# The second expert layer's routing for seven of eight chunks of tokens, made inside the last pass of a recurrence

## The reference: what is computed

```python
x = x + _L0_attn_a_ref(_layernorm(x), ...)       # retention
x = x + _L0_ffn_ref(_layernorm(x), Wg, bg, w1, w2)   # experts, first time
x = x + _L0_attn_b_ref(_layernorm(x), ...)       # recurrence
x = x + _L0_ffn_ref(_layernorm(x), Wg, bg, w1, w2)   # experts, second time
```

```python
logits = t @ Wg.T + bg
topw, topi = jax.lax.top_k(jax.nn.softmax(logits), 2)
```

## Time and profile before

| what | value |
|---|---|
| time, median of 3 runs | 1299.88 us (1298.88 to 1305.9) |
| the profiled execution's own time | 1299.14 us |
| its span (first to last instruction) | 1297.3 us |
| mean granted PE clock | 0.942 of full |
| busy: PE, DVE, ACT, POOL | 1118.2, 853.3, 616.5, 599.1 us |
| the last full pass of the recurrence (n = 7), from its first masked scores | about 976 to 1005 us |
| ffn2: start, first gather, first expert matmul | 1021.6, 1063.8, 1068.6 us |

### The profile page before, as it was taken

One profiled execution on the slowest core, in us unless ns is written; L12 is line 12 of the kernel. 1 busy time (PEld: TensorE's weight loads), 2 busy tenths in 40 slices (PEclk: granted clock), 3 DMA queues, 4 the chain that ended last, 5 costly groups with the idle time before them and its releaser, 6 DMA issues. The chain is left out here.

```text
span 1297.3 us, 35874 instructions
## 1 busy us (share of the span) xinstructions
PE 1118.2 (86%) x14378; PEld 828.5 (64%) x14378; DVE 853.3 (66%) x1705; ACT 616.5 (48%) x1165; POOL 599.1 (46%) x604
## 2 busy tenths in 40 slices
PE   6999999874999997879898999999886748999960
PEld 4778787653788887545555555555555537888860
DVE  4667776677555555576978888697763584555547
ACT  4666666352333332254665747366552523333324
POOL 4556565222577774506244151524411215777750
PEclk9999999996999998999999999899997969999985
DMA  8342320059533333000010101010000484333338
GB/s 304 125 156 75 123 84 34 2 196 328 178 103 103 105 101 97 33 34 4 34 35 3 34 4 34 3 35 3 3 2 3 164 322 134 103 106 103 102 119 343
DMA packets 50687, 125.54 MB, mean 97 GB/s; under 512 B 7648, under 2 KB 26848, under 8 KB 47712
## 3 DMA queue, kind: packets, MB, share of 16 engines
q1 hardware_dynamic: 36896, 86.00, 18.4%
q0 software_dynamic: 13632, 37.24, 8.8%
HBM read 79.44 MB, written 43.78 MB: 95 GB/s over the span
## 5 line engine op out<-in xcount | busy, mean ns | idle before, releaser
L1154 POOL DMA_INDIRECT ffn_xs<-xn_rows,ffn_from_row x142 | 138.4, 975 | 109.9 <-DVE ffn_second_y_at L1558 67.2
L1162 POOL DMA_INDIRECT y_rows<-ffn_ys,ffn_to_row x142 | 140.2, 987 | 68.3 <-DVE ffn_ys L1599 36.0
L1328 PE MATMUL ffn_ps_h<-ffn_w_high,ffn_moved 128*128 x568 | 158.1, 400 | 1.3 <-DVE ffn_moved L1591 1.3
L1213 ACT ACTIVATE ffn_silu_g<-ffn_ps_h 128x256 f32<-128x256 f32 x142 | 54.5, 384 | 207.0 <-PE ffn_ps_h L1328 207.0
L1586 DVE TENSOR_TENSOR ffn_act_in<-ffn_silu_g,ffn_ps_h 128x256 f32<-128x256 f32 x142 | 59.7, 420 | 122.3 <-ACT ffn_silu_g L1213 122.3
L1341 PE MATMUL ffn_ps_o<-ffn_w,ffn_moved 128*128 x852 | 134.6, 294 | 0.0
L1591 DVE TENSOR_TENSOR ffn_moved<-ffn_ps_t,ffn_moved 128x512 fp32r<-128x512 f32 (+1 forms) x152 | 99.6, 656 | 47.8 <-ACT ffn_moved L1217 47.7
L1341 PEld LDWEIGHTS ffn_ps_o<-ffn_w,ffn_moved 128*128 128x128 f32 x852 | 110.0, 189 | 0.3
L1915 POOL TENSOR_TENSOR rec_mixed_k<-rec_mixed_k,rec_xnt 128x512 f32<-128x512 f32 x16 | 17.5, 1091 | 195.1 <-DVE rec_mixed_k L2721 195.1
L1328 PEld LDWEIGHTS ffn_ps_h<-ffn_w_high,ffn_moved 128*128 128x128 f32 x568 | 97.5, 190 | 14.4 <-issue 2.0
L1217 ACT ACTIVATE ffn_moved<-ffn_ps_t 128x512 fp32r<-128x512 f32 (+1 forms) x152 | 86.9, 572 | 39.0 <-PE ffn_ps_t L1318 30.1
(11 more groups left out here) (359 smaller groups left out, 2718.0 us busy)
## 6 DMA issues: line engine op xcount, KB each, us to landing
home<-y_rows SPq DMA_DIRECT2D x30, 512.0 KB, 4.7
w_split<-home SPq DMA_DIRECT2D x24, 512.0 KB, 3.7
ffn_w_high<-w_split SPq DMA_DIRECT2D x8, 1024.0 KB, 9.3
ffn_w_low<-w_split SPq DMA_DIRECT2D x8, 1024.0 KB, 10.4
ffn_w<-w_split SPq DMA_DIRECT2D x8, 1024.0 KB, 13.2
home<-in_f_w SPq DMA_DIRECT2D x12, 512.0 KB, 5.8
xn_rows<-home SPq DMA_DIRECT2D x12, 512.0 KB, 11.3
out<-x SPq DMA_DIRECT2D x8, 512.0 KB, 5.7
```

The lines of the kernel that those rows point to most:

```text
L1154: pool.indirect_dma_start(xs[:, n % SLOTS, :], None, xn_rows[:], bass.IndirectOffsetOnAxis(ap=from_row[:, n:n + 1], axis=0)) \
L1162: pool.indirect_dma_start(y_rows[:], bass.IndirectOffsetOnAxis(ap=to_row[:, m:m + 1], axis=0), ys[:, m % SLOTS, :], None).then_inc(ys_stor ...
L1213: act.activation(silu_g[:, u % 2, :], ps_h[:, n % H_BANKS, 0:FF], ACT.Silu).then_inc(silu_ready, 1)
L1328: mm = pe.matmul(ps_h[:, n % H_BANKS, :], one_pass(moved[:, (n - X_AHEAD) % 3, part, 0, k, :]), one_pass(w1[w_part][k][:, bass.ds(e, E_COL ...
```

## The change

Routing is now made for chunks 0 to 6 in pass 7 of the recurrence, between the steps of chunk 7, and the second expert layer keeps only chunk 7 and the choice of the second half (`ROUTED` is 7 in ffn2, 0 in ffn1). The gate matrix and two small constants live in tiles that outlast the blocks; the small routing tiles of ffn2 lie in `home` (`route_views`). In ffn1 two small loads are added for the constants. `choose_two` holds the 14 operations of `choose`, unchanged. Of the experts' block the diff's core is this:

```diff
-        ROOTS = (0, 1, 3, 5, STEPS)
+        ROOTS = (ROUTED, STEPS) if ROUTED else (0, 1, 3, 5, STEPS)
...
+                AHEAD = 2 if ROUTED else 4
+                if not ROUTED:
+                    sp.dma_start(constants[:, 0:width(F_GATE)], d["f_gate"]).then_inc(consts_loaded, 16)
+                    sp.dma_start(gate_consts[:, 0:NE], d["f_gate"][:, KT * 32:KT * 32 + NE]).then_inc(consts_loaded, 16)
+                    sp.dma_start(gate_consts[:, NE:2 * NE], d["f_route"][:, P:P + NE]).then_inc(consts_loaded, 16)
                 sp.dma_start(constants[:, width(F_GATE):], d["f_route"]).then_inc(consts_loaded, 16)
-                for tile, array in first_loads[:4]:
+                for tile, array in first_loads[:AHEAD]:
                     sp.dma_start(tile, array).then_inc(w1_loaded, 16)
-                for n in range(STEPS):
+                for n in range(ROUTED, STEPS):
...
+                if ROUTED:
+                    take_logits(0)
+                    act.wait_ge(ln_offset, 2)
...
                 norm(XN_STEPS + 1)
...
-                for n in range(STEPS):
+                for n in range(STEPS - ROUTED):
                     transpose_step(n)
...
+                if ROUTED:
+                    dve.wait_ge(logits_in_psum, 1)
+                    scaled_logits(dve, logits, rstd, ps_o[:, 0, :], 0, ROUTED * UNROLL).then_inc(logits_scaled, 1)
+                    choose(ROUNDS - 1)
```

In the recurrence the new steps are `early_transposes` (PE, 8 transposes of a chunk of `x`), `early_products` (PE, the logits of chunks 0 to 3 or 4 to 6), `early_logits` (PE, 4 transposes back), `early_roots` (POOL, behind `add_near_23` of chunk 7), `take_xt` and `take_logits` (ACT, out of PSUM), `early_norm` (DVE, 4 tiles), `early_scale` and `early_choose` (DVE), and 7 stores on SP:

```diff
+                def early_transposes(c):
+                    pe.wait_ge(x_added, c + 1)
...
+                def early_products(n):
+                    first, last = EARLY_ROUNDS[n]
+                    bank = (even, odd)[n]
+                    pe.wait_ge(early_xt_ready, last)
...
+                def early_logits(n):
...
+                def early_roots():
+                    pool.memset(r_of["expo"], -0.5).then_inc(first_constants, 1)
...
+                    for first, last in ((0, 2), (2, 4), (4, LAST)):
+                        part = slice(first * CT, last * CT)
+                        pool.tensor_tensor(r_of["rstd"][:, part], r_of["vare"][:, part], r_of["expo"][:, part], ALU.pow) \
+                            .then_inc(ln_rstd, 1)
...
+                def take_xt(c):
...
+                def early_norm(c):
...
+                for n in range(LAST):
+                    sp.wait_ge(xn_ready, CHUNKS * CT + n + 1)
+                    sp.dma_start(xn_rows.rearrange("(i p) c -> p i c", p=P)[:, n * CT:(n + 1) * CT, :], early_xn[n]) \
+                        .then_inc(early_xn_stored, 16)
+                sp.wait_ge(early_xn_stored, 16 * LAST)
...
-                        keep_going(odd[:, 0, :], 13)
+                        keep_going(odd[:, 0, :], 6)
...
+                    if n == LAST:
+                        early_norm(4)
+                        early_norm(5)
+                        early_norm(6)
+                        early_scale(0)
+                        early_choose()
```

More of the change, by code:

```diff
@@ L1167, in take_logits @@
                 def take_logits(n):
+                    rows = slice(0, 32 if ROUTED else P)
                     act.wait_ge(logits_t_in_psum, n + 1)
@@ L1406, in norm, with scale @@
                     op.then_inc(xn_ready, 1)
[L1408 to L1412 removed]
+                def scale(n):
                     dve.wait_ge(logits_in_psum, n + 1)
```

362 lines of the change are left out of this document (267 added, 95 removed).

## The result

The changed kernel takes 1294.05 us in the median of nine executions, the kernel before 1305.43 beside it; the ratio is 0.993, with a 95% interval from 0.9911 to 0.9949. That is faster, by some 9 us (6.7 to 11.6), where the forecast said 12. The time itself lies just outside its range (1283 to 1294), and part of that is the starting point: the forecast counted from 1299.14 and a median of three executions, 1299.88, where nine gave 1305.43. Twelve us from there would have been 1293. A second series gave 1296.87 for 1303.98, 0.9942 (0.9921 to 0.9964).

What follows compares the result with a forecast made beforehand. The second head was bound by the order of small steps; in pass 7 no engine was full. Terms -10.0, +1.7, -5.0, +0.5, +0.8 sum to -12.0 us from 1299.14: 1287.1, said as 1287, range 1283 to 1294.

Steps and rivals of the forecast that it cites:

- Head of the second layer: Second expert layer, first transpose to choice: 9.89 us for 21.16, taken as -10.0 us (-11.3 to -9.2).
- PE work inserted: Pass 7: transposes and products put into PE's gaps at full clock overhang them by +1.7 us.
- The clock in pass 7: Pass 7: filled gaps bring PE's clock to pass 6's 1.00, so steps shorten: -5.0 us (-6.0 to 0).
- Rival B: Pass 7's clock does not stay up, the -5.0 falls away: 1296 us; chance 0.18.
- Powers beside the scan: Pass 7: three POOL powers run where DVE scans the states, one may wait: +0.5 us (0 to 2.4).
- First expert layer: First layer's head: two more loads ahead of the last constant delay the choice, +0.8 us (0 to 1).
- Transfers: Early stores in pass 7 stay hidden and second-layer weights land before use: 0 us, at most +1.5.
- Rival C: Second layer: weight loads behind chunk 7's store become the bound, landing after their use: 1291 us; chance 0.10.
- rival D: Pass 7: all inserted PE work and the pass run at the low clock, +4.2 us: 1303; chance 0.07.

Runs made afterwards that it cites:

- w2_late: Changed kernel with the last two weight loads waiting for the fourth gather's landing instead of the first, in both expert layers; 1292.63 us, 0.9897 of the kernel before.
- shift32: Changed kernel with 32 more dummy transposes in the first expert layer, behind the count product; 0.996 of the kernel before.
- no_stores: Changed kernel without the seven stores of normalised rows in pass 7, so the second layer gathers old rows; 0.9933 of the kernel before.
- keep13: Changed kernel with 13 dummy transposes ahead of the last output, as before, instead of 6; 0.9941 of the kernel before.
- shift16: Changed kernel with 16 more dummy transposes in the first expert layer, behind the count product; 0.9976 of the kernel before.
- before_fill: Kernel before with 76 dummy transposes in pass 7, in the places of the new work, and nothing else; 1.0002 of the kernel before.
- before_pad: Kernel before with 76 dummy transposes behind the last expert matmul, so only PE's stream is longer; 1.0005 of the kernel before.
- pool_consts: Changed kernel without the two extra first-layer loads, POOL copying the 16 columns from the loaded constants; 0.9934 of the kernel before.
- head_filled: Changed kernel with dummy transposes: 13 ahead of the last output, 10 behind it, 8 ahead of the second layer's logits product; 0.9938 of the kernel before.
- w2_head: Changed kernel with the last two weight loads held for the fourth gather and dummy transposes around last output and second head; 1288.63 us, 0.989 of the kernel before.

## Why the forecast was right in sign and wrong in size

*Head of the second layer, -10.0 (-11.3 to -9.2).* Right in its working, and the size was -11.5 in both traces, a little beyond the range: the steps took 9.70 us for the 9.89 added up. The 1.3 us taken for half clock didn't come there, since the low stretch fell into the output just ahead; where it fell into the head (w2_late, shift32, no_stores, keep13, shift16) it cost 1.4 to 2.5.

*PE work inserted, +1.7.* The places were right: gaps of 1.34 and 2.09 took their blocks (0.31 us left of the first), and products and block between outputs 1 and 2 pushed the latter (1001.85 to 1004.73, 2.9 us for 1.99 of gap). Alone it can't be read off, since the stops lie between.

*The clock in pass 7, -5.0, and the gaps taken as room for work.* This is the step that failed, and not at the clock. "PE's work there looks like pass 6, where the clock was 1.00" came true to the digit. That the steps then end earlier by 5 us did not: PE stood 3.5 us without instructions (before: 0 and 0.36), and the last output lost 1.7 more at half clock, with seven dummy transposes fewer ahead of it. With +1.7 for the inserted work this makes -5.0 + 3.5 + 1.7 + 1.7 = +1.9, against +1.2 measured for pass 7. before_fill shows this term with the inserted work and nothing else, 45.79 us, and before_pad bears out the clock's price (42.76 us with gaps left open). What the forecast put at nothing, without a reason, is the time in which PE's own instructions come. Rival B had the right result (nothing gained) with the wrong cause: the swinging clock that the Trainium skill describes ("TensorE: Matmul & The Clock Gate", section "A second HAM failure mode: psum-queue depth-cycling") isn't there, with 1.00 over 30 us of short waits in both traces; four other kernels with the change (pool_consts, head_filled, w2_late, w2_head) have 0.94 there, from one low stretch of 3.4 us each.

*Powers beside the scan, +0.5.* Too dear. The scan ran inside the powers at its own length, as these rows of POOL and DVE show; it was two plain two-input operations of DVE beside POOL's additions that grew, 0.80 and 0.92 for 0.29, off the path.

```profile
986.26 5.57 POOL L2046 TENSOR_TENSOR home<-home 128x8 f32<-128x8 f32 x3 [3.57 <-DVE home L46]
```

```profile
990.12 1.36 DVE L2967 TENSOR_TENSOR_SCAN rec_state<-rec_s_mult,rec_s_add 128x576 f32<-128x576 f32 x1
...
1009.84 2.54 POOL L2038 TENSOR_TENSOR rec_y<-rec_y,rec_y_near 128x512 f32<-128x512 f32 x2 [18.02 <-ACT rec_y L2239]
1010.46 0.80 DVE L895 TENSOR_TENSOR home<-home,gate_consts 128x128 f32<-128x128 f32 x1
1011.29 0.29 DVE L898 TENSOR_REDUCE home<-home 128x16 f32<-128x128 f32 x1
1011.61 0.92 DVE L900 TENSOR_TENSOR home<-home 128x128 f32<-128x128 f32 x1
```

The rule of the Trainium skill that was weighed there ("SBUF — State Buffer", section "SBUF: two separate sides") is not borne out by the scan; the two DVE operations, 0.80 and 0.92 us long, speak for it.

*First expert layer, +0.8.* Right for the head in place and size where the clock was full (0.6 to 0.9); the 1.1 of the two pairs is a low stretch, so there the number agreed by luck. What the forecast lacked is the loop, +3.3: it worked out the second layer's transfers and never asked what a choice one us later does to the order of loads and gathers in the first (the fourth gather waited for 3.60 us instead of 0.71). This is the second step that failed, the sentence "up to 1 us of delay reaches the choice": it doesn't end at the choice.

*Transfers, 0.* Right in the second layer: first expert matmul 25.0 us behind the count product for 25.6, no wait for weights. *Rival C* did not come, *rival D* neither.

In sum, by the pairs of traces: head 2 -11.5 for -10.0, pass 7 +1.2 for -2.8, the first layer +4.4 for +0.8, the passes +3.3 (not assigned) and the rest -1.2 for 0: -3.8 for -12.0. The median moved by 7 to 11, so the -12.0 looks better against the medians than its parts deserve. The range ended too low because every bound stood on the stretch that the change touches, and on a median of three.

## What to carry to other kernels

Before a gap of PE is counted as room for work, ask whether PE's instructions will come fast enough: in groups of small matmuls, a gap may be the time in which the next ones are loaded. A term like "the clock recovers" is best made by itself first, with dummy work in the old kernel. And a wait that names an early event ("the first gather has landed") leaves the order of two queues to a shift of one us upstream; releasing the loads by the gather that is needed first took one number and brought more than half as much as the whole change (0.0033 to 0.0045 of the time for 0.0058 to 0.007).

## What the runs showed of the hardware

PE stops inside groups of small matmuls for 0.2 to 2.5 us with no releaser in the profile, at distances of some 126 matmuls and multiples of it (252, 124, 253). Their places are fixed in the count of PE's matmuls and not in the program's steps (16 transposes far upstream: the same count, 16 matmuls earlier in the group; 32: a stop of 2.14 us gone). 124 of 127 stops of 0.3 us and more end 1.2 to 1.6 us after a 16 KB transfer of the queue "instruction" has landed. Over all traces the sum is 2.9 to 6.5 us in the kernel before and its kin with gaps, 6.5 to 13.6 where pass 7 is dense (counting each of 0.15 us and more). Seven stores of 512 KB in pass 7 changed nothing in it (3.34 without, 3.54 and 3.34 with them). What decides the size of one stop stays open: at one and the same count (5247) it was 0.54 to 2.14 us with the stream of before.

Around a pause of PE of 2.06 us between two blocks, a fall of the clock to 0.50 met the output ahead of it (5.41 for 3.72) in three of ten traces, the product behind it (3.3 to 3.6 for 1.90) in five, and neither in two. With dummy work on both sides neither was slow, in three traces of three; work on one side alone isn't shown to do anything.
